# The second layer norm's scale and shift moved from ScalarE to VectorE in a two-layer graph kernel

## What is computed

```python
h = jnp.maximum(_layernorm(x, axis=-1), 0.0)
x = x + _L0_gnn_ref(h, adj, ...)     # layer 0: attention with 4 heads
h = jnp.maximum(_layernorm(x, axis=-1), 0.0)
x = x + _L1_gnn_ref(h, adj, L1_gnn_W, L1_gnn_a)   # layer 1: graph attention
# layer 0
scores = clip(q @ k.T / sqrt(32), -10, 10); scores = where(mask == 0, -10, scores)
attn = softmax within each chunk of 128 keys; ctx = sum over the 8 chunks of attn @ v
out = layernorm(ctx @ Wo.T + bo + h) * gamma + beta
# layer 1
Wh = h @ W; e = leaky_relu(Wh @ a1 [:, None] + Wh @ a2 [None, :])
h_prime = softmax(where(adj or eye, e, -inf)) @ Wh; elu(h_prime)
```

## Time and profile before

| | |
|---|---|
| median of 3 runs | 720.74 us |
| lowest, highest | 719.30, 720.92 us |
| profiled execution | 718.64 us |
| its span | 716.9 us |
| DVE busy | 662.4 us (92%) |
| ACT busy | 651.6 us (91%) |
| PE busy | 651.6 us (91%) |
| POOL busy | 526.8 us (73%) |

### The profile page before, as it was taken

The page is one execution under the profiler, slowest core; times in us unless marked ns, Lnnn a source line. Parts: engine busy times, 40 slices in busy tenths (PEclk is TensorE's granted clock), DMA queues, the critical chain, the costliest instruction groups (busy, mean ns, idle before and its releaser), DMA issues.

```text
span 716.9 us, 13598 instructions
## 1 busy us (share of the span) xinstructions
PE 651.6 (91%) x4393; PEld 348.5 (49%) x4393; DVE 662.4 (92%) x1165; ACT 651.6 (91%) x1140; POOL 526.8 (73%) x629
## 2 busy tenths in 40 slices
PE   4389999999899999998999999999999999994976
PEld 2333333344345563546436464557336463564865
DVE  3599999999999999998999999999999999989976
ACT  6399999998999999998999999999999999987655
POOL 2324648656589877978789578998778779998864
PEclk9799999999999999999999999999999999998888
DMA  8742132324121225233222234222222312010111
GB/s 282 236 157 103 60 118 104 103 89 161 63 84 46 93 71 176 75 104 111 80 77 81 90 104 152 91 77 71 83 96 78 114 53 96 23 53 16 51 52 46
DMA packets 58647, 68.53 MB, mean 96 GB/s; under 512 B 5328, under 2 KB 35024, under 8 KB 58576
## 3 DMA queue, kind: packets, MB, share of 16 engines
q1 hardware_dynamic: 57568, 67.39, 27.9%
q10 hardware_dynamic: 1008, 0.26, 0.2%
HBM read 21.50 MB, written 12.58 MB: 48 GB/s over the span
## 4 chain that ended last, share of the span: by engine, by line
PE 39%; ACT 18%; DVE 17%; POOL 10%; issue 10%; DMA 5%; SPq 3%; DVEq 0%; ACTq 0%; POOLq 0%
PE work L1726 11%; PE score L1643 9%; DVE probs L1451 8%; PE work L1660 7%; PE work L1654 6%; ACT score L1296 6%; POOL ring L1248 3%; ACT ring L1364 3%; DVE ring L1542 2%; ACT inverse L1303 2%; ACT inverse L1306 2%; DVE scaled L1477 2%; DVE near_row L1521 2%; SPq L1098 1%; PE work L1618 1%
## 5 line engine op out<-in xcount | busy, mean ns | idle before, releaser
L1451 DVE SCALAR_TENSOR_TENSOR probs<-score,cap 128x1024 f32<-128x1024 f32 x256 | 307.9, 1214 | 11.6 <-ACT score L1296 9.0
L1296 ACT ACTIVATE score<-score 128x1024 f32<-128x1024 f32 x256 | 259.1, 1022 | 6.7 <-PE score L1643 5.2
L1643 PE MATMUL score<-query_stack,key_stack 128*128 128x512 f32 x512 | 188.3, 452 | 14.1 <-DVE probs L1451 10.3
L1223 POOL TENSOR_TENSOR gathered<-gathered,scaled 128x512 f32<-128x512 f32 x112 | 150.3, 1342 | 44.2 <-DVE scaled L1477 41.7
L1248 POOL TENSOR_TENSOR ring<-ring,see_t 128x512 f32<-128x512 f32 x112 | 134.5, 1211 | 22.4 <-DVE ring L1542 21.9
L1643 PEld LDWEIGHTS score<-query_stack,key_stack 128*128 128x128 f32 x512 | 78.6, 189 | 135.8 <-DVE probs L1451 104.7
L1660 PE MATMUL work<-probs,ones 128*32 128x512 f32 x1024 | 135.3, 604 | 1.0 <-DVE scaled L1477 0.4
L1654 PE MATMUL work<-probs,value 128*32 128x512 f32 x1024 | 133.6, 600 | 0.2
L1726 PE MATMUL work<-wh,ring 128*128 128x130 f32 x896 | 110.6, 279 | 12.8 <-ACT ring L1364 11.9
L1726 PEld LDWEIGHTS work<-wh,ring 128*128 128x128 f32 x896 | 107.1, 194 | 23.9 <-issue 16.1
L1364 ACT ACTIVATE ring<-ring,wh 128x512 f32<-128x512 f32 x128 | 90.0, 729 | 9.7 <-POOL ring L1248 7.7
(11 more groups left out here) (117 smaller groups left out, 844.5 us busy)
## 6 DMA issues: line engine op xcount, KB each, us to landing
query_stack<-parts SPq DMA_DIRECT2D x64, 256.0 KB, 2.6
key_stack<-parts SPq DMA_DIRECT2D x56, 256.0 KB, 2.5
x_in<-in_x SPq DMA_DIRECT2D x16, 256.0 KB, 3.2
h_kept<-x_in SPq DMA_DIRECT2D x16, 256.0 KB, 2.6
res<-h_kept SPq DMA_DIRECT2D x16, 256.0 KB, 2.9
h<-in_x SPq DMA_DIRECT2D x16, 256.0 KB, 3.4
x_kept<-res SPq DMA_DIRECT2D x16, 256.0 KB, 2.2
gat_x<-x_kept SPq DMA_DIRECT2D x32, 128.0 KB, 2.3
```

What stands on the lines that cost most here:

```text
L1223: nc.gpsimd.tensor_tensor(sums, sums, scaled[:, k % SCALED], ALU.add).then_inc(gathered_step, 1)
L1296: nc.scalar.activation(some, some, ACT.Exp, scale=DH ** -0.5).then_inc(exp_done, 1)
L1451: nc.vector.scalar_tensor_tensor(out=probs[:, group_of(b, k) % KEPT], in0=score[:, h:h + GROUP, :], scalar=LOW, in1=caps.broadcast_to([P, ...
L1643: last = nc.tensor.matmul(score[:, head, :], key_stack[:, head, chunk * P:(chunk + 1) * P], query_stack[:, head, half * HALF:(half + 1) * ...
```

## The change

`apply_z` moves from ACT to DVE and becomes four `tensor_scalar` (multiply by the scale, add the shift), without the Relu. The Relu is applied where ACT copies the transposed tile out of PSUM, which is the same since a transpose moves values only. The waits are the same: DVE now waits for `shift_done`, and PE for `normed`. All places of all five tables and the banks are new; which steps each table holds is the same, but for the 16 `apply_z`. The line numbers of the changed kernel are higher by up to 8.

```diff
@@ scalar @@
-                    nc.scalar.copy(h1_t[:, side], work[:, bank, :]).then_inc(work_read[bank], 1)
+                    nc.scalar.activation(h1_t[:, side], work[:, bank, :], ACT.Relu).then_inc(work_read[bank], 1)
...
-                elif name == "apply_z":
-                    apply(f"z{k}", b + 1, h1[:, k], res[:, k], ACT.Relu)
@@ vector @@
+                elif name == "apply_z":
+                    _, _, _, scale, shift = norm[f"z{k}"]
+                    dve.wait_ge(shift_done[f"z{k}"], b + 1)
+                    for t in range(TILES):
+                        last = nc.vector.tensor_scalar(h1[:, k, t, :], res[:, k, t, :], scale[:, t:t + 1],
+                                                       shift[:, t:t + 1], ALU.mult, ALU.add)
+                    last.then_inc(normed[f"z{k}"], 1)
@@ table of ACT, batch 5 (one of eight) @@
-        "apply_z": [1420, 4845],
-        "turn_hidden": [2323, 5224],
...
```

More of the change, by code:

```diff
@@ new lines @@
+        "apply_x": [751, 1165],
+        "first_weights": [906],
+        "cast": [1022, 1580, 1874, 2201],
+        "turn_x": [1117, 1733],
+        "key": [1321, 2296],
+        "mask": [1380, 1471, 1782, 2018, 2109, 2355, 3718, 4539],
+        "weights": [1563, 2688],
+        "query": [1675, 2538],
+        "value": [1969, 2712],
+        "exp": [2446, 2596, 2765, 2903, 3150, 3292, 3535, 3627, 3863, 3955, 4302, 4394, 4630, 4775, 4975, 5120,
+            5520, 5661, 5856, 6001, 6201, 6305, 6606, 6697, 6996, 7087, 7451, 7542, 7755, 7868, 8120, 8212],
@@ new lines @@
+    2: {
+        "apply_x": [-13836, -12750],
+        "turn_x": [-10494, -9528],
+        "query": [-8533, -3684],
+        "key": [-7128, -5348],
+        "value": [-5587, -4227],
+        "exp": [-4531, -4416, -4164, -4069, -3776, -3626, -3430, -3167, -2964, -2824, -2444, -2353, -2105, -1937,
+            -1666, -1459, -1251, -1143, -828, -683, -479, -267, -10, 214, 461, 711, 906, 1195, 1403, 1650, 1854,
+            2119],
+        "log_sum": [-3958, -3318, -3066, -2610, -2155, -1837, -1368, -878, -592, -113, 606, 803, 1083, 1804, 2211,
+            2662],
+        "inverse": [-3855, -3256, -2560, -2261, -2014, -1512, -1304, -737, -63, 82, 852, 1030, 1349, 2314, 2712,
+            2820],
+        "apply_y": [3778, 8303],
+        "turn_hidden": [6052, 10218],
+        "to_row": [10432, 10573],
+        "wh": [12339, 12379, 12702],
+        "base_row": [13263, 13311],
+        "gat_exp": [13704, 14020, 14136, 14677, 14739, 14893, 15150, 15447, 16388, 16450, 16512, 16775, 17265,
+            17419, 18225, 18341],
+        "below": [16014, 16891, 19813, 20562],
+        "above": [16067, 17036, 19866, 20615],
+        "exp_below": [16264, 17183, 20129, 21206],
+    },
@@ new lines @@
+        "moments_x": [510, 640],
+        "bias_row": [1092],
+        "cast": [1112, 1370, 2020, 3221],
+        "see": [1173, 1207, 1822, 1856, 2080, 2114, 7424, 7458],
+        "key": [1430, 2408],
+        "edges": [1496, 1626, 1890, 2148, 2278, 3515, 4296, 5379],
+        "query": [1756, 3013],
+        "probs": [2568, 2709, 2900, 3079, 3281, 3402, 3646, 3759, 4010, 4183, 4426, 4539, 4741, 4914, 5093, 5266,
+            5647, 5772, 5973, 6112, 6312, 6425, 6724, 6837, 7138, 7251, 7562, 7675, 7866, 7979, 8231, 8344],
```

1245 lines of the change are left out of this document (604 added, 641 removed).

## The result

The changed kernel takes 745.8 us (median of four runs, 742.8 to 751.1) against 720.4 for the kernel before (four runs, 719.3 to 720.9): a ratio of 1.036, interval 1.029 to 1.043. The forecast was 724.0 with a range of 713 to 732, so the sign was right and the size was not. The profiled execution took 748.2 us, with a span of 746.5; before it was 716.9.

The account below looks back on a forecast made before the run. A ring of PE, ACT and DVE, with DVE and ACT alternately last, was taken to bound the long stage. 10.4 + 5.6 + 1.0 - 13.7 = +3.3 us on 720.7 gave 724.0 us, range 713 to 732.

Parts of the forecast that it names:

- DVE becomes the only bound: Long stage: DVE's load grows by more than ACT's lateness gives back; 724.0 us, chance 0.42.
- Step 1: ACT: loses the second layer norm's application, 26.4 us busy; the Relu copy adds at most 0.3; ACT falls to about 625.
- Step 2: DVE: gains 64 tensor_scalar in 16 groups of four, 0.65 us a group, 10.4 us in all.
- Step 3: DVE's new groups: POOL instructions hold them up, 0.35 us a group, 5.6 us; bounds 2.8, 11.1 and 17.1.
- rival B: DVE's new groups: heavy blocking, POOL breaks in between the four, 14 us in place of 5.6; 733 us, chance 0.10.
- Step 4: DVE's new groups: the wait for POOL's rstd moves from ACT to DVE; 1.0 us, between 0 and 3.
- Step 5: Long stage: the lighter ACT returns all 13.7 us of DVE's idle that ended with ACT; bounds 0 and 21.0.
- Rival D: Long stage: faster, 18 of DVE's 21.0 us idle return, not only those ended by ACT; 716 us, chance 0.26.
- Step 6: All engines' instruction orders, laid out anew: 0 us, with 4 us either way.
- the sign against this step: Last 77 us: a difference of more than 2 us there would show the new orders' 0 us wrong.

Follow-up runs that it names:

- one for four, constants: The changed kernel with one tensor_scalar over 128x512 in place of each group's four, constants 1 and 0 for scale and shift: 714.2 us, ratio 0.994.
- accumulating form: The changed kernel with each of the four tensor_scalar also writing its accumulator, the shift left out of what it writes: 721.4 us, ratio 1.002.
- four with constants (second): The changed kernel with constants 1 and 0 for scale and shift in the four tensor_scalar, run again for a profile: 735.4 us, ratio 1.022.
- two broadcasts: The changed kernel with each group's four tensor_scalar replaced by two 128x512 tensor_tensor, scale and shift as broadcasts: 740.9 us, ratio 1.029.
- eight accumulating: The changed kernel with eight accumulating tensor_scalar a group, four of them into a spare tile, shift left out: 746.4 us, ratio 1.039.

## Why the prediction was wrong

Put together, span = DVE's busy time + DVE's idle time:

| kernel | DVE busy us | DVE idle us | span us |
|---|---|---|---|
| before | 662.4 | 54.5 | 716.9 |
| new lists, on ACT | 661.5 | 63.9 | 725.4 |
| new lists, on POOL | 666.9 | 51.3 | 718.2 |
| old lists, on POOL | 669.8 | 58.5 | 728.3 |
| one for four, constants | 673.6 | 36.4 | 710.0 |
| accumulating form | 681.7 | 36.9 | 718.6 |
| four with constants (second) | 694.1 | 40.4 | 734.5 |
| old lists, on DVE | 697.7 | 54.3 | 752.0 |
| two broadcasts | 698.7 | 40.4 | 739.1 |
| eight accumulating | 702.8 | 41.8 | 744.6 |
| after | 703.3 | 43.2 | 746.5 |
| scalar_tensor_tensor, accumulating | 704.2 | 43.0 | 747.2 |
| scalar_tensor_tensor | 704.4 | 41.5 | 745.9 |

With the new lists and the group on DVE, the idle time stays at 36 to 43 us, whatever DVE runs, and the span goes with its busy time, a little more than one for one (from one for four to after, DVE gains 29.7 us and the span 36.5). The reading that DVE becomes the only bound was right for these lists. It does not hold for the old ones, where DVE idles for 54.3 us with the group on it, as before.

- **Step 1** (ACT loses 26.4 us, the Relu is free): nearly. The Relu copy takes 594 ns against 585, 0.1 us in all, and the busy times of ACT's groups add up to about 30 us less than before. But the busy line, which counts overlapping neighbours once, fell by 18.0 us only, to 633.6 and not 625. That an ACT that waits more often has fewer neighbours that overlap is likely, but was not tested. The forecast took a sum of group times off a busy time without overlaps.
- **Step 2** (10.4 us; a group of 0.65): wrong in size, 17.6 us; the group takes 1.10. The row of cap was the same operation between the same memories, but with constants, and for constants 0.65 was right (0.62 measured). The row with scalars from SBUF, L1564 at 1.2 us a group, stood in the earlier trace rows as the upper bound and was the near one.
- **Step 3** (5.6 us; 0.35 a group): the step that failed. The mechanism was right, its size was 24.1 us (1.5 a group, 0.38 an instruction), above the highest bound of 17.1. That bound took one loss a group, and the one that let all 64 lose took 0.17 us for each; the eight instructions at 27.39 that were not broken into the earlier trace rows were read as a sign that a series is safe. It isn't: in the forms tested here each instruction gives the turn to whichever POOL instruction is ready, so a group loses up to four of POOL's. The row for this was the one quoted for rival B: three L1547 in a row took 4.08 us, where one alone took 0.67, so each of a series lost near 0.7 us. B had the right mechanism with 14 us for it; at 733 us it was too low as well.
- **Step 4** (1.0 us for rstd): at its lower bound, the idle time before the group is 0.1 us and none of it is rstd's.
- **Step 5** (all 13.7 us of idle come back): near in size, but not for the reason given. DVE's idle went from 54.5 to 43.2, 11.3 us, and to 36.9 in the accumulating form. Rival D's guess that more than ACT's share returns holds there, 17.6 us, but it needed the light group. With the old lists an ACT that is some 20 us lighter gave nothing back: DVE's idle is 54.3 us with the group on DVE and 58.5 with it on POOL. With the new lists and the group on POOL instead of on ACT it falls by 12.6 us (63.9 to 51.3). So the relief of ACT pays only together with the new lists, and the prediction had put it down to ACT's load alone.
- **Step 6** (new lists 0, 4 either way): too narrow. They cost 7 us with the group on ACT and save 8 with it on DVE (753.9 to 745.8) and 9 with it on POOL (728.7 to 720.1); they pay once ACT is light. The last stretch, from the end of the last probs on, grew by 4.1 us (80.8 to 84.9), where 2 us was the sign against this step; but it is 81.2 us in the accumulating form, so the growth comes with the holding and not with the lists. The range of 713 to 732 needed both this and the blocking to be wider.

The measured sum: 17.6 + 24.1 - 0.8 for DVE's other groups and overlaps, less 11.3 of idle, makes +29.6, against +3.3. Of the 26.3 us between, step 3 has 18.5 and step 2 has 7.2. The right sign owes something to luck. DVE's load was forecast at 662.4 + 16.0 = 678.4 us; the kernels on either side of it, with 673.6 and 681.7 us, took 714.2 and 721.4 us, against 719.6 for the kernel before beside them. An estimate between the two gives 718 us for the load of the forecast, and not 724.

One thing stays open. From the accumulating form to the kernel after, DVE gains 21.6 us and the span 27.9, so 6.3 us of idle come on top. PE's granted clock between 400 and 500 us is 0.97 in the kernel after and 1.00 in the accumulating one, with PE idle 8.3 us of these 100 and 3.0 there, and PE's busy time over the span is 11.5 us longer. Whether the lower clock makes the extra idle or follows from it is not shown: no run holds the clock and changes the rest.

## What to carry to other kernels

Before moving work to DVE where POOL is busy, count instructions, not only us, unless their form is one that POOL does not hold: with POOL busy for 70% of the span, four short ones from SBUF to SBUF lost 1.5 us a group here, and one for four 0.4 us. Look for the nearest row by its operands too, scalars from memory or constants, not by operation and memory alone. And where the sum gives a few us to a mechanism that a rival prices at two and a half times that, the range has to reach the rival.

## What the runs showed of the hardware

- A one-tensor tensor_scalar that accumulates is not held by POOL (391 to 426 ns over 64), while the plain one is (332 to 1316) and so is an accumulating scalar_tensor_tensor (335 to 1359).
- Reading scale and shift from SBUF, and not constants, costs a tensor_scalar of 128x128 0.12 us (0.62 to 1.10 us for four), when nothing else runs on POOL.
- At the place shown POOL isn't slowed: its two ring products take 2.27 us beside the plain form and 2.28 beside the accumulating one, and DVE alone pays.
- POOL can be held in turn, and for a whole series. With the new lists and apply_z on POOL, an instruction of apply_z, 449 ns in the median, took 1917 ns from 672.01 us on, beneath three tensor_tensor of DVE that ran at their full pace. The 3.48 us of the earlier trace rows are the same case, beneath eight. What decides whether a series is broken into or keeps POOL waiting is open:

```profile
671.15 3.21 POOL L1200 TENSOR_SCALAR h<-res,small 128x128 f32<-128x128 f32 x4
671.85 1.93 DVE L1555 TENSOR_TENSOR ring<-ring,see_t 128x512 f32<-128x512 f32 x3
```

- An undisturbed group of four on POOL takes 1.74 us, where DVE alone needs 1.10 and ACT needed 1.65.
